# Softmax of two self-attention layers: ScalarE makes the exponentials head by head, with the maximum as bias and sums collected on the way

## The reference, cut to what matters

```
q = (x @ Wq + bq).reshape(B, S, H, hd).transpose(0, 2, 1, 3)      # B=8, S=64, H=16, hd=16
k = (x @ Wk + bk).reshape(B, S, H, hd).transpose(0, 2, 1, 3)
v = (x @ Wv + bv).reshape(B, S, H, hd).transpose(0, 2, 1, 3)
scores = jnp.einsum('bhqd,bhkd->bhqk', q, k) * scale
scores = jnp.where(allowed, scores, NEG_INF)                      # L0: causal
attn = jax.nn.softmax(scores, axis=-1)
out = jnp.einsum('bhqk,bhkd->bhqd', attn, v)
out = out.transpose(0, 2, 1, 3).reshape(B, S, D)
return out @ Wo + bo
...
x = x + _L0_attn_ref(_layernorm(x, axis=-1), L0_attn_Wq, ...)
x = x + _L3_attn_ref(_layernorm(x, axis=-1), L3_attn_Wq, ...)     # no biases; ALiBi slopes are added to the scores
```

## Time and profile before

| what | value |
| --- | --- |
| median of 3 runs | 2827.24 us (2825.17 to 2831.76) |
| the profiled execution | 2830.46 us, its span 2828.6 us |
| TensorE matmuls busy | 2606.4 us (92%) |
| VectorE busy | 1656.9 us (59%) |
| ScalarE busy | 1110.7 us (39%) |
| L0 attention, first scores taken to last residual | 1177.53 to 1210.30 us |
| L3 attention, the same | 2716.20 to 2748.60 us |

### The profile page before, as it was taken

One profiled execution on the slowest core, in us unless ns is written; L12 is line 12 of the kernel. 1 busy time (PEld: TensorE's weight loads), 2 busy tenths in 40 slices (PEclk: granted clock), 3 DMA queues, 4 the chain that ended last, 5 costly groups with the idle time before them and its releaser, 6 DMA issues. The chain is left out here.

```text
span 2828.6 us, 44290 instructions
## 1 busy us (share of the span) xinstructions
PE 2606.4 (92%) x17687; PEld 1797.9 (64%) x17687; DVE 1656.9 (59%) x3773; ACT 1110.7 (39%) x2061; POOL 611.3 (22%) x312
## 2 busy tenths in 40 slices
PE   6999999999999999789999987998998779999978
PEld 3566666666666666556667653555895447888846
DVE  5657575666656555445656645994553361187655
ACT  3343434443443433124555545871232342311123
POOL 2041313122221210000000000992001051155402
PEclk9999999999999999989999999999999999999979
DMA  5324333332333222041101000114696538733210
GB/s 175 91 62 130 76 98 81 105 101 73 101 86 101 73 50 50 14 158 60 48 25 48 1 9 16 53 53 170 243 347 247 196 102 309 267 118 124 69 44 9
DMA packets 87956, 295.83 MB, mean 105 GB/s; under 512 B 9024, under 2 KB 46598, under 8 KB 80838
## 3 DMA queue, kind: packets, MB, share of 16 engines
q1 hardware_dynamic: 83942, 284.53, 31.3%
q0 software_dynamic: 2784, 7.61, 0.7%
q10 hardware_dynamic: 1024, 0.86, 0.1%
HBM read 281.42 MB, written 11.02 MB: 103 GB/s over the span
## 5 line engine op out<-in xcount | busy, mean ns | idle before, releaser
L1984 PE MATMUL L_xattn_bank<-L_xattn_keys_tok,L_xattn_probsT 128*128 128x257 f32 x1664 | 412.8, 392 | 1.1 <-ACT L_xattn_probsT L1803 0.2
L1913 PE MATMUL L_xattn_wide<-L_xattn_keys_feat,weights_a 128*128 128x512 f32 (+2 forms) x1024 | 390.0, 524 | 6.5 <-ACT L_xattn_keys_feat L1823 3.6
L1984 PEld LDWEIGHTS L_xattn_bank<-L_xattn_keys_tok,L_xattn_probsT 128*128 128x128 f32 x1664 | 300.6, 190 | 91.2 <-issue 40.9
L1913 PEld LDWEIGHTS L_xattn_wide<-L_xattn_keys_feat,weights_a 128*128 128x128 f32 x1024 | 186.8, 192 | 155.2 <-issue 129.1
L1561 DVE COPY L_xattn_k_normed<-L_xattn_wide 128x833 f32<-128x833 f32 (+1 forms) x128 | 131.1, 1024 | 196.3 <-PE L_xattn_wide L1913 196.1
L1797 ACT ACTIVATE L_xattn_scores<-L_xattn_scores,L_xattn_neg_max 128x897 f32<-128x897 f32 x128 | 126.4, 1035 | 257.1 <-DVE L_xattn_neg_max L1586 257.1
L1581 DVE CUSTOM_DVE_ANT_0 L_xattn_scores<-L_xattn_wide,L_xattn_mask_row 128x897 f32<-128x897 f32 x128 | 134.9, 1088 | 105.9 <-issue 105.9
L3150 POOL TENSOR_TENSOR L_attn_state<-L_attn_state,L_attn_C_rows 128x1024 f32<-128x1024 f32 x80 | 190.5, 2415 | 26.4 <-DVE L_attn_state L3039 25.0
L2201 DVE CUSTOM_DVE_ANT_0 L_xattn_scores<-L_xattn_banks,L_xattn_mask 128x512 f32<-128x512 f32 (+1 forms) x256 | 131.4, 570 | 92.1 <-issue 92.1
L3039 DVE TENSOR_TENSOR_SCAN L_attn_state<-L_attn_decay,L_attn_banks 128x1024 f32<-128x1024 f32 x80 | 176.1, 2261 | 15.5 <-PE L_attn_banks L3245 15.5
L3914 PE MATMUL L_ffn_banks<-L_ffn_slot_features,L_ffn_expert_w 128*128 128x128 f32 x1440 | 168.4, 277 | 3.0 <-DVE x_tok L3709 3.0
(11 more groups left out here) (558 smaller groups left out, 4650.0 us busy)
## 6 DMA issues: line engine op xcount, KB each, us to landing
L_xattn_k_scale<-L_xattn_k_scale_rows SPq DMA_DIRECT2D x128, 417.0 KB, 4.8
L_ffn_expert_w<-in_x_L_ffn SPq DMA_DIRECT2D x16, 2056.0 KB, 9.0
L_xattn_ctx_feat<-in_ctx_feat SPq DMA_DIRECT2D x11, 1601.0 KB, 7.2
L_ffn_expert_w<-in_x_L_ffn SPq DMA_DIRECT2D x17, 1024.0 KB, 5.7
L_ffn_expert_w<-in_x_L_ffn SPq DMA_DIRECT2D x15, 1028.0 KB, 5.8
L_xattn_keys_tok<-in_ctx_tok SPq DMA_DIRECT2D x8, 1536.0 KB
L_attn_C_rows<-L_attn_c_rows SPq DMA_DIRECT2D x24, 512.0 KB, 3.6
weights_a<-in_ctx_feat SPq DMA_DIRECT2D x6, 1601.0 KB, 10.4
```

What stands on the lines that cost most here:

```text
L1913: last = nc.tensor.matmul(wide[:, 2 * h + c, 0:n], wk[:, k, p * P:(p + 1) * P], xnT[b % 2][:, k, a:a + n], start=(k == 0), stop=(k == KT - 1))
L1984: last = nc.tensor.matmul(bS[:, 0:D + 1], pT[:, c, a, :, :].rearrange("p h q -> p (h q)"), xn[b % 2][:, t, :], start=(i == 0), stop=(i == ...
```

## The change

For tiles 0, 1 and 3 (`BY_HEAD`) `shift` makes only the reduction, negated, and no subtraction. `exponentials` makes 16 operations of 128 x 64, one per head, each with that head's negated maximum as a per-partition bias and with an accumulator output that leaves the head's sum in `sm`. `divide` leaves out the reduction of sums. Tile 2 stays as it was. Two lists are written in another order: VectorE does `shift(2)` and `shift(3)` ahead of `divide(0)`, and `residual(0)` and `residual(1)` ahead of `divide(3)`; ScalarE does `exponentials(2)` ahead of `copy_turned(0)`. TensorE's list is unchanged.

```diff
+    BY_HEAD = (0, 1, 3)
...
                 def shift(t):
                     dve.wait_ge(s_taken, t + 1)
+                    if t in BY_HEAD:
+                        nc.vector.tensor_reduce(mx[:, t, :], sc[t][:, :, :], AX.X, ALU.max, negate=True).then_inc(shifted, 1)
+                        return
                     chain(nc.vector.tensor_reduce(mx[:, t, :], sc[t][:, :, :], AX.X, ALU.max))
...
                 def divide(t):
                     dve.wait_ge(exp_ready, t + 1)
-                    chain(nc.vector.tensor_reduce(sm[:, t, :], sc[t][:, :, :], AX.X, ALU.add))
+                    if t not in BY_HEAD:
+                        chain(nc.vector.tensor_reduce(sm[:, t, :], sc[t][:, :, :], AX.X, ALU.add))
...
                 shift(1)
                 scores_taken(2)
                 scores_taken(3)
+                shift(2)
+                shift(3)
                 divide(0)
-                shift(2)
                 divide(1)
-                shift(3)
                 attended(0)
                 divide(2)
+                residual(0)
                 attended(1)
-                residual(0)
+                residual(1)
                 divide(3)
-                residual(1)
                 attended(2)
...
                 def exponentials(t):
                     act.wait_ge(shifted, t + 1)
-                    nc.scalar.activation(sc[t][:, :, :], sc[t][:, :, :], ACT.Exp).then_inc(exp_ready, 1)
+                    if t not in BY_HEAD:
+                        nc.scalar.activation(sc[t][:, :, :], sc[t][:, :, :], ACT.Exp).then_inc(exp_ready, 1)
+                        return
+                    for a in range(16):
+                        last = nc.scalar.activation(sc[t][:, a, :], sc[t][:, a, :], ACT.Exp, bias=mx[:, t, a:a + 1],
+                                                    accum_out=sm[:, t, a:a + 1])
+                    last.then_inc(exp_ready, 1)
...
                 exponentials(0)
                 exponentials(1)
+                exponentials(2)
                 copy_turned(0)
-                exponentials(2)
                 even_heads(0)
```

## The result

The changed kernel takes 2838.79 us (median of 10 runs, 2834.41 to 2844.23) against 2827.55 us (10 runs, 2818.18 to 2834.11): a ratio of 1.0045 with a 95% interval of 1.0033 to 1.0056, so 9.3 to 15.8 us slower. The profiled execution took 2837.67 us with a span of 2835.9, 7.3 us more than the span before.

What follows compares the result with a forecast made beforehand. The prediction took VectorE to bound both attention stages up to the last tile's product. Stage losses of 3.0 and 3.3 us plus 0.7 each for TensorE's clock made +7.7 us, 2834.9 us at the median; range 2829.7 to 2840.3.

Steps and rivals of the forecast that it cites:

- A head's cost: ScalarE's step per head's exponential: 0.24 us plus 0.09 for the accumulator's read, 0.33 us; a tile 5.4 us against 1.06.
- free read: Rival on ScalarE: the accumulator's read costs nothing, 0.24 us per head; about +3.5 us, 2830.7 us; chance 0.13.
- without overlap: Rival on ScalarE: the read overlaps nothing, 0.52 us per head, a tile 8.3 us; +21.6 us, 2848.8 us; chance 0.05.
- VectorE's gain: Three subtractions and three reductions of sums, some 1.24 us each, leave VectorE: 7.4 us in each stage.
- The path in L0: First attention stage: merge and residual of tile 1 delay the last division; last turn at 29.7 against 26.7 us, +3.0 us.
- the tail: Last tile's chain from turn to residual, running alone from engine to engine; the same before and after.
- the 0.5 us put in for it: In L3 the filling matmuls end later, so the second turn starts 0.5 us later than in L0; stage +3.3 us.
- the walk: Stepping through the engines' written-out lists with step lengths from the trace; gave +3.0 us in L0, +3.3 with L3's later turn.
- The clock: TensorE's clock falls to 0.50 in the gap before `project(1)`, slowing it and `residual(1)`: +0.7 us for each stage.
- rival 4: The low clock lasts to the stage's end, adding 2.9 us in place of 0.7: +12.1 us, 2839.3 us; chance 0.10.
- the prediction's own sign of being wrong: Wrong if a tile of heads takes under 4.5 or over 6 us, VectorE is not idle, or outside layers change over 2 us.

Runs made afterwards that it cites:

- the second comparison: The unmodified changed kernel measured again against the kernel before: 2843.39 us (7 runs), ratio 1.0039 (1.0025 to 1.0053).
- no_accumulator: Changed kernel without accumulator outputs, VectorE summing all four tiles by a reduction again; ratio 1.0035 (1.0024 to 1.0046) against the kernel before.
- lists_alone: Changed kernel's reordered lists with no tile made by heads; ratio 1.0033 (1.0020 to 1.0045) against the kernel before.
- gap_filled: Changed kernel with three filling matmuls between `turn_probs(2)` and `project(1)`; ratio 1.0023 (1.0013 to 1.0033) against the kernel before.
- heads_old_lists: Changed kernel, tiles 0, 1 and 3 by heads, with both lists of before; ratio 1.0023 (1.0007 to 1.0039) against the kernel before.
- Delay_control: Kernel before with three extra VectorE reductions behind the last residual of each attention stage; 2831.95 us (11 runs), ratio 1.0014 (1.0002 to 1.0025).
- tuned_0_2: Changed kernel with tiles 0 and 2 by heads and VectorE's and ScalarE's lists rewritten; 2815.11 us, ratio 0.9955 (0.9938 to 0.9972) against before.
- tile3_whole: Changed kernel with tile 3 made whole, as tile 2; ratio 1.0027 (1.0017 to 1.0037) against the kernel before.
- old_lists_filled: Tiles 0, 1 and 3 by heads in the lists of before, plus two and three more filling matmuls; ratio 1.0013 (1.0000 to 1.0026) against before.
- tuned_lists_alone: Lists rewritten for tiles 0 and 2 by heads, but no tile by heads; 2828.94 us, ratio 1.0000 (0.9985 to 1.0016) against before.

## Why the prediction came out as it did

The forecast, +7.7 us or 2834.9, was in the right direction and of the right size, and the median of 2838.79 lies in its range. For the mechanism the stages count, and there it held to a few tenths in L0. That the time lies in the range is in part luck: in the second comparison the median is 2843.39, above the range's end of 2840.3 (its kernel before was 2.3 us slower, too).

- **A head's cost.** Forecast 0.33 us, from two rows of other shapes; measured 0.33 (exponential 335 ns, read 188 ns, overlapping). Right, and shown by no_accumulator. The rivals with a free read or without overlap (0.24, 0.52) are out.
- **VectorE's gain.** 7.4 us a stage forecast, 7.1 measured. It came through nowhere: VectorE waited it away, 2.46 us for the second reciprocal, 3.28 for `attended(1)`. The forecast put it at a step of 1.24 us for each of the six operations; their busy time sums to a little less.
- **The path in L0.** Second turn at 16.4, merge of tile 1 at 25.1, last turn at 30.4 with the clock's 0.7: measured 16.2, 24.9 and 30.3. Right, and the tail behind it is 6.08 us long before and after. In L3 the second turn was forecast at 16.9 and came at 16.2, 16.8 and 16.8, so the 0.5 us put in for it came true in two of three traces.
- **The lists.** That the residual ahead of the last division costs was part of the walk, and lists_alone shows that the lists cost when VectorE is the bound. What I had not seen is that the heads and the lists are not a sum: in the traces they are +4.6 and +7.8 us alone in L0, together +3.65. The walk at full clock has the same order, +1.5 and +5.9 alone and +3.0 together. The ratios do not show it: +2.0 to +11.0 and +5.7 to +12.7 us alone, +9.3 to +15.8 together.
- **The clock.** This is the term that was mis-sized. That it falls in the gap was right in all six stages traced, and gap_filled shows both the cause and the price (0.96 us for each stage, forecast 0.7). The 0.7 came from a turn of 1.78 us that was only in part at the low clock; wholly at it, a turn takes 1.97 (heads_old_lists). And the forecast has one slow passage, up to `project(1)` and `weigh(2)`, and rival 4 with a chance of 0.10 has all of it slow to the end. In L3 two of three traces lay between: turn 3 and `project(2)` were slow too, 1.23 us more, and `weigh(3)` and `project(3)` at full clock. With it the two stages cost 8.3 us on the mean and not 7.7.
- **The sum.** Forecast +7.7, measured +9.3 to +15.8 and in the second comparison +7.1 to +15.0. The stages explain 7.1 to 9.1, 8.3 on the mean. The two ratios stand for +12.7 and +11.0 us, so some 3 to 4 us are left; their intervals let it be anything from nothing to 7.5. This stays open. Delay_control speaks against a knock-on cost, and the rest of the program scatters by 10 us over the 14 traces, more than the amount in question. So the prediction's own sign of being wrong, layers outside that change by more than 2 us (they changed by +0.2 in the first trace, +4.2 and -0.8 in the others), cannot be read from single traces. One other layer was longer in all three traces of the changed kernel, L2's cross-attention (87.3 to 87.5 us from its first layer-norm instruction to the next layer's, against 85.9 and 84.8 before), but it took 85.9 in lists_alone, whose stages were the longest of all, and 87.1 to 87.4 in four others; that this belongs to the change is not shown.

## What to carry to other kernels

Splitting one operation into 16 is paid at the fixed cost of each: here 4.3 us of ScalarE for 2.4 of VectorE a tile. As far as these two sets of lists show, it is worth that only where the receiving engine has a hole of that length and no short step of another tile waits behind it; in the traces the heads cost 4.6 us a stage in the lists of before and won 6.5 in the tuned ones; by the walk at full clock the two are 1.1 to 1.5 and 5.0. A walk over the written-out lists, with each step's length from the trace, comes within a few tenths where TensorE's clock does what was assumed (L0 of the changed kernel, gap_filled, tuned_0_2). Where it did otherwise the walk missed a stage by 1.1 to 2.3 us (lists_alone, heads_old_lists, tile3_whole, old_lists_filled, tuned_lists_alone), as much as some of the differences that it was to tell apart. Filling matmuls count as work in that walk: they stand in TensorE's list, and at the low clock they take twice their time.

## What the runs showed of the hardware

The clock can stay low although TensorE is at work again: behind a gap in L3 it was busy for 2.74 of 3.4 us at 0.51, and the clock was still 0.50 in the next 3.4 us. In other traces it was back at full in that place (0.99 in L0 of the first). The same 3.56 us without work left the first turn at 1.10 us in one kernel's trace and at 1.97 in another's. A filling instruction of 512 columns is 0.46 us at full clock (2.74 for six) and 0.91 at the low one (3.62 for four), so a fill meant to keep the clock up is twice as long just when it comes too late. The accumulator's read, 188 ns long, costs only 0.09 us of ScalarE's time at 64 elements. At 1601 it is followed by the next exponential 0.09 us after its start, too, but no run has that shape without the read.
